# The last block's router moves into the other block's shared expert, and the weight splits move behind it

## What is computed

```python
shared = jnp.einsum('ts,sh->th', jax.nn.silu(x @ sw_gate) * (x @ sw_up), sw_down)   # SI = 704
logits = x @ router_w.T                                                            # E = 8 experts
probs = jax.nn.softmax(logits.astype(jnp.float32), axis=-1)
top_w, top_i = jax.lax.top_k(probs, TOP_K)                                         # TOP_K = 2
top_w = top_w / jnp.sum(top_w, axis=-1, keepdims=True)
combine = jnp.sum(jax.nn.one_hot(top_i, E) * top_w[..., None], axis=1)
h = jax.nn.silu(jnp.einsum('th,ehi->eti', x, w_gate)) * jnp.einsum('th,ehi->eti', x, w_up)
expert_out = jnp.einsum('eti,eih->eth', h, w_down)
routed = jnp.einsum('eth,te->th', expert_out, combine)
shared_out = jax.nn.sigmoid(x @ shared_gate_w)[:, None] * shared
return (routed + shared_out)
```

## Time and profile before

| | |
|---|---|
| median of three runs | 642.36 us |
| the profiled execution | 641.28 us |
| its span, first to last instruction | 639.5 us |
| mean granted TensorE clock | 0.913 |
| TensorE busy | 536.0 us, 84% |
| VectorE busy | 411.9 us, 64% |
| ScalarE busy | 258.9 us, 40% |
| GpSimd busy | 109.7 us, 17% |

### The profile page before, as it was taken

One profiled execution on the slowest core, in us unless ns is written; L12 is line 12 of the kernel. 1 busy time (PEld: TensorE's weight loads), 2 busy tenths in 40 slices (PEclk: granted clock), 3 DMA queues, 4 the chain that ended last, 5 costly groups with the idle time before them and its releaser, 6 DMA issues.

```text
span 639.5 us, 8171 instructions
## 1 busy us (share of the span) xinstructions
PE 536.0 (84%) x2464; PEld 425.0 (66%) x2464; DVE 411.9 (64%) x1249; ACT 258.9 (40%) x463; POOL 109.7 (17%) x133
## 2 busy tenths in 40 slices
PE   2835358999469999999989998999879799999690
PEld 1423335587347687887677886888667699999580
DVE  6886653789873898974687872417646366766136
ACT  3711344433445414456424335111641256666103
POOL 1600002200002232002204000040001334444200
PEclk9977679999768999999989997999969989999996
DMA  8961000000010002010001000010050324443523
GB/s 303 421 159 33 0 2 0 1 0 34 33 33 1 0 35 67 34 34 33 1 2 66 0 34 33 2 67 20 14 178 28 109 81 127 120 135 102 196 108 131
DMA packets 29485, 44.42 MB, mean 69 GB/s; under 512 B 3147, under 2 KB 24139, under 8 KB 29099
## 3 DMA queue, kind: packets, MB, share of 16 engines
q1 hardware_dynamic: 24451, 32.95, 16.2%
q0 software_dynamic: 3408, 9.38, 3.9%
q10 hardware_dynamic: 1584, 1.57, 0.9%
HBM read 27.55 MB, written 16.34 MB: 69 GB/s over the span
## 4 chain that ended last, share of the span: by engine, by line
PE 54%; DVE 33%; ACT 5%; issue 4%; DMA 2%; POOL 0%; DVEq 0%; POOLq 0%; ACTq 0%; SPq 0%
PE psum L709 10%; PE psum L710 10%; PE psum L711 9%; PE psum L750 8%; PE psum L776 5%; PE psum L719 3%; PE psum L825 3%; PE psum L946 2%; DVE SM L1304 2%; DVE rt L985 2%; DVE rt L984 2%; PE psum L916 1%; PE psum L899 1%; DMA YF<-y_routed 1%; DVE XC L1178 1%
## 5 line engine op out<-in xcount | busy, mean ns | idle before, releaser
L621 ACT ACTIVATE SM<-psum 128x512 f32<-128x512 f32 (+1 forms) x56 | 33.1, 594 | 137.6 <-PE psum L711 103.6
L1304 DVE TENSOR_TENSOR SM<-SM,psum 128x512 f32<-128x512 f32 (+1 forms) x56 | 38.1, 683 | 63.7 <-ACT SM L621 63.5
L497 POOL DMA_INDIRECT x_dispatched<-XN,dest x32 | 32.9, 1027 | 184.7 <-DVE XN L1371 176.2
L750 PE MATMUL psum<-WOU,SM 128*128 128x256 f32 x256 | 60.2, 380 | 0.3 <-DVE SM L1304 0.3
L776 PE MATMUL psum<-WQKV,HT 128*128 128x512 f32 (+1 forms) x128 | 50.7, 549 | 6.8 <-ACT GA L608 3.3
L488 POOL TENSOR_TENSOR OG<-QKV,hvec 128x256 f32<-128x256 f32 x16 | 13.3, 833 | 243.9 <-ACT IG L563 224.9
L750 PEld LDWEIGHTS psum<-WOU,SM 128*128 128x128 f32 x256 | 48.1, 189 | 9.2 <-DVE SM L1304 1.0
L506 POOL DMA_INDIRECT y_routed<-GO,g_dest x39 | 37.7, 968 | 56.8 <-ACT GO L684 56.5
L750 PE MATMUL psum<-SDN,SM 128*128 128x256 f32 (+1 forms) x192 | 44.8, 382 | 2.7 <-DVE SM L1304 2.6
L776 PEld LDWEIGHTS psum<-WQKV,HT 128*128 128x128 f32 x128 | 26.5, 212 | 29.4 <-issue 24.7
L750 PEld LDWEIGHTS psum<-SDN,SM 128*128 128x128 f32 (+1 forms) x192 | 35.8, 189 | 10.2 <-DVE SM L1304 4.1
(11 more groups left out here) (271 smaller groups left out, 1331.0 us busy)
## 6 DMA issues: line engine op xcount, KB each, us to landing
XG<-x_dispatched SPq DMA_DIRECT2D x39, 130.0 KB, 2.5
YF<-y_routed SPq DMA_DIRECT2D x2, 2048.0 KB, 10.9
RUPR<-rup SPq DMA_DIRECT2D x1, 2816.0 KB
X<-x SPq DMA_DIRECT2D x4, 512.0 KB, 6.7
x_after_attention<-X SPq DMA_DIRECT2D x4, 512.0 KB, 2.8
QKV<-x ACTq DMA_DIRECT2D x3, 512.0 KB, 3.5
y_shared<-SH SPq DMA_DIRECT2D x3, 512.0 KB, 2.9
SHF<-y_shared SPq DMA_DIRECT2D x1, 1536.0 KB, 9.6
```

The costliest lines, as they stand in the source:

```text
L497: nc.gpsimd.indirect_dma_start(XD[:, :], bass.IndirectOffsetOnAxis(dest[:, i, old + j:old + j + 1], 0), XN[:, j, :], None).then_inc(dispat ...
L621: nc.scalar.activation(SM[0:rows, g % 3, 0:tb], p_pair(n)[0][0:rows, 0:tb], ACT.Silu).then_inc(silu_ready, 1)
L750: last = nc.tensor.matmul(p_down[:, j // 2, (j % 2) * D:(j % 2 + 1) * D], SM[0:rows, g % 3, j * P:(j + 1) * P], weight[0:rows, m, :], star ...
L1304: nc.vector.tensor_tensor(SM[0:rows, g % 3, 0:tb], SM[0:rows, g % 3, 0:tb], value_rows(n, rows)[:, 0:tb], ALU.mult).then_inc(hid_ready, 1)
```

## The change

Block 3's `xt`, `route`, `choose` and `rank` move from behind `shout` (2) into the shared expert of block 2, after its parts 4 to 8. For that, block 3's transposed tokens go to banks 0 and 1 (`p_token`) and to the buffers of the MLP's input, H2H and H2L (`token_parts`), which are free by then; `gate` is doubled. The eight `rsplit` move from block 2's shared expert into block 3's, two behind each of its parts 1 to 4. Waits follow: `xt` (3) on ScalarE waits for the MLP's last up-product, `sdn` (3,0) for SH of block 2 rather than for the router's copy. GpSimd's entries in the table of places are renumbered.

```diff
         norms = {0: [("sum", b, 1)], 1: [("sum", b, 2)], 2: [("x2", b, 0)], 3: [("x2", b, 1)]}
-        if b > 0:
-            pieces = {3: [0, 1], 4: [2, 3], 5: [4, 5], 6: [6], 7: [7]} if b == NB - 1 else {}
-            order += weave(shared(b - 1), {**norms, **{i: norms.get(i, []) + [("rsplit", b, m) for m in ms] for i, ms in pieces.items()}})
-        else:
+        if 0 < b < NB - 1:
+            order += weave(shared(b - 1), norms)
+        elif b == 0:
             order += [s for part in norms.values() for s in part]
-        order += [("xt", b, 0), ("route", b, 0), ("choose", b, 0)]
-    b = NB - 1
-    return order + weave(shared(b), {0: [("choose", b, 1)], 1: [("choose", b, 2)], 2: [("rank", b, 0), ("choose", b, 3)]})
+        if b < NB - 1:
+            order += [("xt", b, 0), ("route", b, 0), ("choose", b, 0)]
+    route = {4: [("xt", b, 0)], 5: [("route", b, 0), ("choose", b, 0)], 6: [("choose", b, 1)], 7: [("choose", b, 2)],
+             8: [("rank", b, 0), ("choose", b, 3)]}
+    order += weave(shared(b - 1), {**norms, **route})
+    pieces = {1: [0, 1], 2: [2, 3], 3: [4, 5], 4: [6, 7]}
+    return order + weave(shared(b), {i: [("rsplit", b, m) for m in ms] for i, ms in pieces.items()})
...
-        p_route = psum[:, 6, 0:J * RP]
...
+        def p_token(b):
+
+            return p_main if b == NB - 1 else p_down
...
-        gate = sb("gate", [P, J])
+        gate = sb("gate", [P, 2, J])
...
+        def token_parts(b):
+
+            return (H2H, H2L) if b == NB - 1 else (XTH, XTL)
...
                     act.wait_ge(xt_psum, b + 1)
-                    if b > 0:
+                    if b == NB - 1:
+                        act.wait_ge(up_psum, done("mup", b, FM - 1))
+                    elif b > 0:
                         act.wait_ge(up_psum, done("hid", b - 1, SMN - 1))
...
                 if stage == "xt":
-                    if b > 0:
+                    if 0 < b < NB - 1:
                         pe.wait_ge(sh_ready, old)
-                    to_features(p_down, lambda j: XN[:, j, 0:D], nj, xn_ready, old).then_inc(xt_psum, 1)
+                    to_features(p_token(b), lambda j: XN[:, j, 0:D], nj, xn_ready, old).then_inc(xt_psum, 1)
...
                         else:
-                            pe.wait_ge(rt_copied, NB)
+                            pe.wait_ge(sh_ready, old)
```

More of the change, by code:

```diff
@@ L632, in at @@
                     act.wait_ge(xt_psum, b + 1)
-                    if b > 0:
+                    if b == NB - 1:
+                        act.wait_ge(up_psum, done("mup", b, FM - 1))
+                    elif b > 0:
                         act.wait_ge(up_psum, done("hid", b - 1, SMN - 1))
                     for c in range(C):
-                        nc.scalar.activation(XTH[:, c, 0:tb], p_down[:, c, 0:tb], ACT.Copy).then_inc(xt_hi, 1)
+                        nc.scalar.activation(token_parts(b)[0][:, c, 0:tb], p_token(b)[:, c, 0:tb], ACT.Copy).then_inc(xt_hi, 1)
                 if (stage, m) == ("choose", 0):
@@ L654, in at @@
                         nc.scalar.activation(SH[:, j, :], p_down[:, j // 2, (j % 2) * D:(j % 2 + 1) * D], ACT.Identity,
-                                             scale=gate[:, j:j + 1]).then_inc(sh_ready, 1)
+                                             scale=gate[:, b % 2, j:j + 1]).then_inc(sh_ready, 1)
             for name, b, m in steps("act"):
@@ L854, in at @@
                         pe.wait_ge(wr_lo, 1)
+                    part_h, part_l = token_parts(b)
                     for j in range(nj):
@@ L857, in at @@
                         for c in range(C):
-                            last = mm3(p_route[:, j * RP:(j + 1) * RP], XTH[:, c, t], XTL[:, c, t], wrH[:, c, :], wrL[:, c, :],
+                            last = mm3(p_token(b)[:, 0, j * RP:(j + 1) * RP], part_h[:, c, t], part_l[:, c, t], wrH[:, c, :], wrL[:, c, :],
                                        c == 0, c == C - 1)
@@ L864, in at @@
                     pe.wait_ge(xt_lo, C * (b + 1))
-                    up_product(stage, b, m, (XTH, XTL),
+                    up_product(stage, b, m, token_parts(b),
                                lambda half, part, c: part["sup"][:, c, sup_cols(m, half)])
@@ L1332, in at @@
                         dve.wait_ge(xt_hi, C * b + c + 1)
-                        nc.vector.tensor_tensor(XTL[:, c, 0:tb], p_down[:, c, 0:tb], f32(XTH[:, c, 0:tb]), ALU.subtract).then_inc(xt_lo, 1)
+                        part_h, part_l = (t[:, c, 0:tb] for t in token_parts(b))
+                        nc.vector.tensor_tensor(part_l, p_token(b)[:, c, 0:tb], f32(part_h), ALU.subtract).then_inc(xt_lo, 1)
                 if stage == "route":
                     dve.wait_ge(rt_psum, b + 1)
-                    nc.vector.tensor_copy(LG[:, 0:nj, :], p_route[:, 0:nj * RP].rearrange("p (j r) -> p j r", r=RP)[:, :, 0:RW]).then_inc(rt_copied, 1)
+                    nc.vector.tensor_copy(LG[:, 0:nj, :], p_token(b)[:, 0, 0:nj * RP].rearrange("p (j r) -> p j r", r=RP)[:, :, 0:RW]).then_inc(rt_copied, 1)
                 if (stage, m) == ("choose", 0):
@@ L1371, in at @@
                     nc.vector.tensor_copy(XN[:, 0:nj, D + 1], top[:, 2, 0:nj]).then_inc(tag_ready, 1)
-                    nc.vector.reciprocal(gate[:, 0:nj], top[:, 0, 0:nj]).then_inc(shared_gate, 1)
+                    nc.vector.reciprocal(gate[:, b % 2, 0:nj], top[:, 0, 0:nj]).then_inc(shared_gate, 1)
                     if b == NB - 1:
```

## The result

The changed kernel takes 638.23 us (median of six runs, 636.61 to 639.45) against 642.34 for the kernel before in the same runs: ratio 0.9934, 95% interval 0.9919 to 0.9948, so 3.3 to 5.2 us faster. 637.0 had been forecast, with a range of 633.6 to 640.2.

The account below looks back on a forecast made before the run. TensorE was taken to bound the kernel, idling mostly for VectorE. Removed waits, less a new 5.8 us wait and 2.6 us of slow restart, ended the shared expert at 502.8 against 508.2: gain 5.4, forecast 637.0 us, range 633.6 to 640.2.

Parts of the forecast that it names:

- The waits ahead of the router: Ahead of block 3's router: TensorE's waits of 1.19, 1.40, 1.66 and 2.01 us go; some 1 us idle at `xt`.
- The router: Block 3's 24 router products: bounds 2.6 and 5.1 us, taken as 2.6 + 0.8 = 3.4, ending at 462.15.
- the clock falls in the router: Rival at block 3's router: one or two `sdn` also run at half clock, 1.7 us each; 639.4 us, 12%.
- The ranks and the table: Behind the rank products: VectorE's 10.6 us, covered by two `hid` (5.6 us), leave TensorE idle 5.8 us.
- The restart: After the table's wait, TensorE restarts at 479.95 us with clock 0.50, costing 2.4 to 3.0 us, taken as 2.6.
- The splits in their new place: In block 3's shared expert: four pairs behind SM (3,1) to (3,4), covered by 2 us at the tightest place.
- GpSimd and SP: Eight indirect DMAs start about 472.5, end at 483 us, landing 17 us before TensorE wants the rows; cost 0.
- The sum: Last shared down-product ends at 502.8 against 508.2 us, gain 5.4; later work unchanged in length; 637.0 us on the median.
- The rival of the missing cover: Rival at the table: `hid` (3,0), (3,1) don't run beneath VectorE's 10.6 us, exposing 5.6; 642.6 us, no change, 5%.
- The clock did not stay at 0.50 to the ranks: Denies the slower rival: clock at 0.50 from the router's start through three `sdn` and the ranks; 643.9 us, 5%.

Follow-up runs that it names:

- e1_splits_only: The kernel before with only the eight weight splits moved into block 3's shared expert, router left in place: 641.37 us against 641.25, ratio 0.9994.
- e3_table_apart: The changed kernel with the group table as a step of its own and the splits placed around it: 628.54 us, ratio 0.9795 to the kernel before.
- e4_filled_wait: The changed kernel with 24 unread products filling TensorE's wait for VectorE's table: 630.23 us, ratio 0.9819 to the kernel before.
- after: The changed kernel itself, in its first profile, with router and splits both moved against the kernel before: 638.23 us, ratio 0.9934.

## Why the prediction was right, point by point

- **The waits ahead of the router.** Gone, as stepped. `hid` (2,5) began at 455.38 and the router at 458.40 us, where 455.6 and 458.75 had been put down. `e1_splits_only` shows that the first two were the splits', and that they come back elsewhere when the router stays.
- **The router.** Taken at 3.4 us, between 2.6 and 5.1; it took 461.18 - 458.40 = 2.78, with the clock at 1.00 to its end. The trace of the kernel before had this price: block 1's router, 297.20 - 294.50 = 2.70 us, all 24 at the full clock, which the prediction overlooked. The 0.8 us added for a low clock inside the router had no counterpart, and the cost lay where the sum had nothing: the clock fell behind it, and the three `sdn` took 7.2 us (461.18 to 468.42) instead of 5.2. Router and `sdn` together are 10.0 us against 8.65 in the sum, 1.4 too few. That is half the rival "the clock falls in the router": its slow `sdn`, without its slow router, and so 1.4 us where it had 2.4. With 12 and 12 products the clock held in four traces of four, with 24 in none of six; block 1's router shows that 24 in one piece can also pass without a fall.
- **The ranks and the table.** From 469.74 to 480.25 us, 10.51 against 10.6. The wait was 5.68 against 5.8. `e3_table_apart` shows this to be the one large thing the change gives back: with the clock behind it, 8.0 us.
- **The restart.** Low for 4.8 us, 481.08 to 485.9. Predicted price 2.6; `e4_filled_wait` measured 2.2 between A and B. From the restart to the end of the down-products it is 22.74 us against 22.8, but two errors cancel in that: at the full clock throughout, in `e4_filled_wait`, the same work took 501.64 - 481.03 = 20.61 us, not 20.2.
- **The splits in their new place.** No wait for SM stands between 481 us and the end of the shared expert, as forecast; SM (3,5) came at 500.1 us, when its down-product wasn't due until about 502.
- **GpSimd and SP.** The eight dispatches ran from 474.52 to 485.2 us, 2 us later than forecast. 1.2 of it is the later end of the ranks; the rest is in the forecast, for before the change the dispatches began 4.78 us after the ranks (488.02 to 492.80), and so they did here (469.74 to 474.52). XG was loaded 16 us before it was wanted.
- **The sum.** B was forecast 5.4 us earlier and came 4.4 earlier; the 1.0 is the 1.4 of router and `sdn` less some 0.4, most of it won before the router (458.40 for 458.75). Time behind B was taken as unchanged. That held from B to C (99.37 and 99.34), but not for the last sums in the two traces, whose length depends on where the clock is low: 13.98 to 16.87 us over all the traces. In the medians the gain, 4.1, is close to the stretch's 4.4. The time fell in the range because the large terms, the waits and the table, were right; that the clock's errors partly cancelled (0.6 us too much in the router against 2.0 too little behind it, 0.4 either way at the restart) was luck.
- **Slower, or no change.** The rival of the missing cover is excluded: both `hid` steps ran under the table. The clock did not stay at 0.50 to the ranks.

## What to carry to other kernels

When a step is moved under other work, count what the cover consists of for every engine: here the 10.5 us of VectorE behind the ranks had 9.1 us of TensorE's work as cover in its old place and 5.6 in the new, and the wait with the clock behind it gave back 8.0 us. A long chain of small instructions on one engine is better cut, so that what the other engine waits for can go between its parts; cutting this one at one place, and placing the splits around it, brought nearly twice the gain of the whole change (7.98 and 4.37 us between A and B). And two moves that each measure as nothing can pay together, when both compete for the same engine in the same stretch.

## What the runs showed of the hardware

- Twenty-four products of 128x10 in one piece, busy without a gap at the full clock, could be followed by a fall to 1.2 GHz under dense products: in `after` 0.8 us after their end, for 3.4 us. Behind block 3's router it came in six traces of six, behind block 1's in seven of thirteen. Two pieces of twelve with a down-product between were followed by none in four traces. What decides between the two at block 1 stays open.
- The clock fell in a wait of 5.7 us and did not when the wait was filled with products. Both traces with the filled wait were also quicker far from the edit than both of the changed kernel (1.6 us between B and C, 2.8 in the last sums); the first was in no trace without filling products, the second was in `e1_splits_only` too, so it isn't shown to be the filled wait's.
- How long a wait was didn't settle whether the clock fell: behind 1.94 us it held, behind 2.01 us in `e1_splits_only` it was at 0.50 from 488 to 490 us.
- A low stretch can be useful where it lies: under the SHF products, ahead of a wait for a DMA, it cost nothing and left the last sums at the full clock (14.08 rather than 15.5 to 16.9 us).
